# Edge rows of a graph network: gathered once per 128 sorted edges and loaded per tile by a table, instead of gathered per tile

## The reference

```
m   = relu(x3[src] @ We1[0:128] + x3[dst] @ We1[128:256] + be1)    # per edge
agg = segment_sum(m @ We2 + be2, dst)                              # per node
out = layernorm(x3 + relu([x3, agg] @ Wn1 + bn1) @ Wn2 + bn2)      # shortened
```

## Time and profile before

| | us |
|---|---|
| time, median of 3 runs | 4746.93 (4742.55 to 4747.23) |
| span of the profiled execution (no other time of it is given) | 7303.0 |
| POOL busy, 2706 instructions | 2658.9 |
| PE busy | 4076.2 |
| DVE busy | 3381.7 |
| ACT busy | 2340.3 |

### The profile page before, as it was taken

The page is one execution under the profiler, slowest core; times in us unless marked ns, Lnnn a source line. Parts: engine busy times, 40 slices in busy tenths (PEclk is TensorE's granted clock), DMA queues, the critical chain, the costliest instruction groups (busy, mean ns, idle before and its releaser), DMA issues. The chain is left out here.

```text
span 7303.0 us, 82736 instructions
## 1 busy us (share of the span) xinstructions
PE 4076.2 (56%) x24237; PEld 3354.5 (46%) x24238; DVE 3381.7 (46%) x7886; ACT 2340.3 (32%) x3120; POOL 2658.9 (36%) x2706
## 2 busy tenths in 40 slices
PE   4332641019981111117989798988672197666655
PEld 2111420007761101106778586858571197665644
DVE  4222540358970000106788776456451076555545
ACT  0000010005640000004555455557461075444433
POOL 4555157730017777770000000000427601444463
PEclk7665865559995555558999898989785598888777
DMA  9400000009970000116658287843444343444432
GB/s 376 155 0 0 0 2 0 0 23 334 368 250 0 0 0 0 28 25 222 232 189 293 96 293 214 296 162 95 132 125 124 97 139 98 132 132 130 130 95 67
DMA packets 364823, 923.20 MB, mean 126 GB/s; under 512 B 114026, under 2 KB 138716, under 8 KB 364531
## 3 DMA queue, kind: packets, MB, share of 16 engines
q1 hardware_dynamic: 214722, 650.09, 26.9%
q10 hardware_dynamic: 58609, 180.13, 6.4%
q0 software_dynamic: 91200, 89.42, 5.2%
HBM read 705.69 MB, written 213.71 MB: 126 GB/s over the span
## 5 line engine op out<-in xcount | busy, mean ns | idle before, releaser
L1741 POOL DMA_INDIRECT edges_halves<-local,gather_idx x832 | 854.9, 1027 | 791.7 <-SPq L372 505.4
L1680 POOL DMA_INDIRECT adj_t<-cell_val,cell_at x832 | 828.6, 996 | 465.2 <-issue 369.9
L862 PE MATMUL ps<-tiles_r,stage_r 128*128 128x512 f32 x2028 | 811.6, 400 | 158.2 <-issue 132.0
L1134 POOL DMA_INDIRECT big<-table,gather_idx x576 | 548.4, 952 | 832.3 <-DVE stage L1284 376.3
L869 PE MATMUL ps<-stage,big 128*128 128x130 f32 x4046 | 520.1, 284 | 370.3 <-issue 354.7
L1134 POOL DMA_INDIRECT x_fm<-table,gather_idx x384 | 370.2, 964 | 959.8 <-DMA table<-cell_at 689.7
L869 PEld LDWEIGHTS ps<-stage,big 128*128 128x128 f32 x4046 | 497.9, 199 | 388.5 <-issue 384.6
L2059 PE MATMUL ps<-big,ident_h 128*128 128x104 bf16 (+1 forms) x2880 | 359.7, 256 | 460.4 <-issue 459.7
L1253 PE MATMUL ps<-big,stage 128*128 x1920 | 356.2, 342 | 352.7 <-issue 189.3
L1319 PE MATMUL ps<-ident,big 128*128 128x128 f32 x260 | 73.3, 377 | 817.2 <-issue 768.2
L2442 DVE TENSOR_TENSOR big<-ps,stage 128x1248 bf16<-128x1248 f32 x192 | 270.7, 1451 | 519.5 <-remote 385.1
(11 more groups left out here) (482 smaller groups left out, 9007.8 us busy)
## 6 DMA issues: line engine op xcount, KB each, us to landing
onehot<-adj_t SPq DMA_DIRECT2D x332, 512.0 KB
big<-adj_t SPq DMA_DIRECT2D x332, 512.0 KB
onehot<-adj_s SPq DMA_DIRECT2D x170, 512.0 KB
adj_t<-rows ACTq DMA_DIRECT2D x13, 6656.0 KB
adj_s<-big ACTq DMA_DIRECT2D x157, 512.0 KB, 5.3
stage<-local_rows SPq DMA_DIRECT2D x120, 512.0 KB
big<-adj_s SPq DMA_DIRECT2D x84, 512.0 KB
x_fm<-adj_s SPq DMA_DIRECT2D x84, 512.0 KB
```

The lines of the kernel that those rows point to most:

```text
L862: nc.tensor.matmul(psum_fm(p, n)[:, 0:cut], upper_rows[:, k, :], tile[:, 0:cut], start=k == 0, stop=False, skip_group_check=True)
L1134: return nc.gpsimd.indirect_dma_start(out, None, table[0:N, :], bass.IndirectOffsetOnAxis(gather_idx[:, t:t + 1], 0))
L1680: nc.gpsimd.indirect_dma_start(out, bass.IndirectOffsetOnAxis(cells[:, c:c + 1], 0), cell_val[:, c:c + 1], None).then_inc(S(name), 16)
L1741: nc.gpsimd.indirect_dma_start(edges_halves, bass.IndirectOffsetOnAxis(slot_at[:, at:at + 1], 0), slot_val[:, at:at + 1], None).then_inc(h ...
```

## The change

All 960 gathers of tiles go. The rows of the table are gathered once for each of the 832 rows of sorted edges, in 52 sets of 16 (`GATHERS`, `GATHERED`), and each set is stored to HBM with one DMA of 1 MB. The first 19 sets (`EARLY`) are gathered beside the attention pass into SBUF of `x_fm`, the other 33 after its last weights are made, into SBUF of `big`, with no wait for the edge loop. In the edge stage SP loads each of the 8 tiles of a chunk with a DMA of its own, 128 x 512 bytes, two chunks ahead. Which set and which row of it a tile has, and how many stores must be done for a chunk, are int16 tables in partitions 1 to 3 of `block_of`; SP reads 1 + 8 + 8 of these values into registers per chunk. The tables are made beside the fifth pass and go through HBM (`tile_rows`) to their three partitions; SP waits for three DMAs at the end of that pass where it waited for one. SP also loads all 832 rows of sorted edges before that pass (`row_from`). All 120 chunks are alike, in order; the ring of rows keeps three slots, with a semaphore for each half.

```diff
-EARLY = 48
-EARLY_PAIRS = EARLY // 2
-DIRECT = CHUNKS - EARLY
-TURN = "DEDEDE"
+SLOTS = 3
+AHEAD = 2
+TURN = 2 * SLOTS
+GATHERED = 16
+GATHERS = EDGE_TILES // GATHERED
+EARLY = 19
...
+            eng.load(block_regs[eng, which], block_of[at:at + 1, bass.ds(CH * c, CH)])
+            return [eng.snap(r, min_val=0, max_val=most) for r in block_regs[eng, which]]
...
                 sp.dma_start(local_rows.rearrange("(g p) e -> p g e", p=P), pair_f).then_inc(S("local_stored"), 16)
-                sp.wait_ge(S("local_stored"), 16)
+                sp.dma_start(tile_rows.rearrange("(v g p) a -> p v (g a)", v=3, p=P), tile_row[:, :, :],
+                             allow_slow_non_contiguous=True).then_inc(S("local_stored"), 16)
+                sp.wait_ge(S("local_stored"), ROWS_IN + 32)
+                sp.dma_start(block_of[1:4, 0:T], tile_rows.rearrange("(v t) a -> v (t a)", v=3)[:, 0:T]
+                             ).then_inc(S("local_stored"), 16)
+                sp.wait_ge(S("local_stored"), ROWS_IN + 48)
...
-            for k in range(EARLY_PAIRS):
+            for k in range(GATHERS):
...
+                if k == EARLY:
+                    pool.wait_ge(S("weight_act"), KT * PASS_TURNS)
                 if k >= 2:
-                    wait(pool, early_stored, 16 * (k - 1))
-                for u in range(2 * CH):
-                    if u == CH // 2 and k > 0:
+                    pool.wait_ge(S("rows_stored"), 16 * (k - 1))
+                out = (early_sets if k < EARLY else late_sets)[k % 2]
+                for u in range(GATHERED):
+                    if u == GATHERED // 2 and k > 0:
                         store(k - 1)
...
-        def edge_pool(pool):
-            wait(pool, table_stored, 16 * GROUPS)
-            pool.wait_ge(S("weight_act"), KT * PASS_TURNS)
-            for k in range(DIRECT):
-                slot = k % HOT
-                if k >= HOT:
-                    pool.wait_ge(S("edge_pre"), 2 * direct_at(k - HOT) + 2)
                 for u in range(CH):
-                    gather(pool, row_ring[slot][:, u, :], (EARLY + k) * CH + u).then_inc(half_landed[2 * slot + u // 4], 16)
...
+            def rows_of(spot):
+                if not (spot.known and spot.i == 0 and spot.h < SLOTS):
+                    wait(sp, S("edge_pre"), 2 * (spot.u - SLOTS) + 2)
+                stored = sp.value_load(block_of[3:4, bass.ds(CH * spot.u + CH - 1, 1)], min_val=16, max_val=16 * GATHERS)
+                sets = tile_blocks(sp, spot.u, "set", 1, GATHERS - 1)
+                row = tile_blocks(sp, spot.u, "row", 2, GATHERED - 1)
+                sp.wait_ge(S("rows_stored"), stored)
                 for u in range(CH):
+                    sp.dma_start(spot.rows()[:, u, :], gathered_rows[bass.ds(sets[u], 1), :, bass.ds(row[u] * P, P)]
+                                 .rearrange("g p e -> p (g e)")).then_inc(landed_sem(2 * spot.slot + u // 4), 16)
+            for h in range(AHEAD):
+                rows_of(Spot(0, h))
             def body(spot):
                 wait(sp, S("hot_turned"), spot.u - 1)
-                sp.dma_start(targets[spot.par], local_rows[bass.ds(CH * spot.chunk, CH), :]...
+                sp.dma_start(targets[spot.par], local_rows[bass.ds(CH * spot.u, CH), :]...
-                if spot.h == 5 and not (spot.known and spot.i == LOOPS - 1):
-                    early(EARLY_SLOTS * (spot.i + 1), 0, spot.u - 4)
...
+                if not (spot.known and spot.i == LOOPS - 1 and spot.h + AHEAD >= TURN):
+                    rows_of(spot.after(AHEAD))
```

More of the change, by code:

```diff
@@ L387, in gnn @@
         targets_landed = [S(f"targets_landed{k}") for k in range(2)]
[L388 to L391, removed]
+        halves_written = [Count(S(f"at_written{k}"), 16 * sum(UNITS[k::2])) for k in range(2)]
+        gathered_in = [S(f"gathered_in{k}") for k in range(2)]
         turned_stored = [S(f"turned_stored{s}") for s in range(RING)]
@@ L445, in gnn @@
         targets = [stage[:, (4 + k) * CH * P:(5 + k) * CH * P] for k in range(2)]
[L446 to L450, removed]
+        assert 6 * CH * P <= NBP * W
+        late_sets = [big[:, NP + k * GATHERED * P:NP + (k + 1) * GATHERED * P] for k in range(2)]
+        slots_at = NP + 2 * GATHERED * P
+        row_ring = [out.rearrange("p (t f) -> p t f", f=P) for out in
+                    [rows_flat[:, CH * P:2 * CH * P]] + [big[:, slots_at + k * CH * P:slots_at + (k + 1) * CH * P] for k in range(2)]]
         HOTS = 3
@@ L974, in pair_locals, with row_sets @@
                 chain(dve)(last)
[L976 to L984, removed]
+            def row_sets():
+                for b, w in enumerate(ROW_SETS):
+                    if w != P:
+                        yield b, b + 1, w
+                yield 0, EDGE_TILES // P, P
@@ new lines, in row_sources @@
+            def row_sources():
+                one = chain(dve)
+                dve.wait_ge(S("local_stored"), ROWS_IN)
+                for lo, hi, w in row_sets():
+                    last = nc.vector.tensor_scalar(row_from[0:w, lo:hi, :], row_from[0:w, lo:hi, :], KEY_BITS, None,
+                                                   ALU.logical_shift_right)
+                one(last)
+                for lo, hi, w in row_sets():
+                    last = nc.vector.tensor_scalar(row_src[0:w, lo:hi, :], row_from[0:w, lo:hi, :], float(N - 1), None, ALU.min)
+                one(last)
@@ L1122, in edge_turns, with edge_pool @@
             turn(LOOPS - 1, True)
[L1123 to L1136 removed]
+        def edge_pool(pool):
             pool.wait_ge(S("pair_flipped"), 2)
@@ L1170, in edge_sp @@
[L1170 to L1180 removed]
+                    r = GATHERED * k + u
@@ L1244, in body @@
                 h = spot.par
-                blk = tile_blocks(pe, spot.chunk)
-                if not spot.x and spot.h == 0:
+                blk = tile_blocks(pe, spot.u)
+                if spot.h == 0:
                     wait(pe, node_kept, GROUPS if spot.nodes_done else spot.i)
@@ L1299, in body @@
                 if not spot.first:
-                    blk = tile_blocks(dve, spot.before().chunk)
+                    blk = tile_blocks(dve, spot.before().u)
                 gathered(spot)
@@ L1572, in _ @@
             end_stage(sp, nc.sync)
+            for k in range(2):
+                wait(sp, halves_written[k], 16 * SLW * SL // 2)
+            slots = edges_halves.rearrange("(r e) a -> r (e a)", e=P)
+            full = EDGE_TILES // P
+            sp.dma_start(row_from[:, 0:full, :], slots[0:full * P, :].rearrange("(g p) e -> p g e", p=P)).then_inc(S("local_stored"), 16)
+            if EDGE_TILES % P:
+                sp.dma_start(row_from[0:EDGE_TILES % P, full, :], slots[full * P:EDGE_TILES, :]).then_inc(S("local_stored"), 16)
             matrix_sp(4, sp)
@@ L1729, in _ @@
             pool.wait_ge(stage_end, ended["first"])
-            halves_written = [Count(S(f"at_written{k}"), 16 * sum(UNITS[k::2])) for k in range(2)]
             def sorted_there(n):
```

201 lines of the change are left out of this document (82 added, 119 removed).

## The result

The changed kernel takes 5097.65 us (median of 4 runs, 5095.81 to 5106.83), the kernel before 4747.08 beside it (4742.55 to 4754.35). The ratio is 1.0742, 95% interval 1.0727 to 1.0757: 350.6 us slower. The prediction was 5185 (4980 to 5420), slower at 0.90.

What follows compares the result with a forecast made beforehand. The prediction took DVE's chain of waits, not gathers, to bound the edge stage before, and SP's queue after. 4746.9 + 434 (edge stage) + 4 (tables and row load), early and late gathers 0, gave 5185 us, range 4980 to 5420.

Steps and rivals of the forecast that it cites:

- edge stage, after: Edge stage of the changed kernel: 120 SP turns of 10.1 us plus the last chunk's rest, 1234 us, +434.
- tables at the end of pass 5: End of the fifth pass: the tables' store and load end 3 to 4 us late; with the row load +4, bounds 0 and 15.
- SP becomes the engine that the stage waits for: Edge stage: SP's turn of 10.1 us (8.9 to 13.1) exceeds DVE's 6.53, so SP's queue holds up the stage.
- SP's turn, 10.1 us: Edge stage, per chunk: destinations load 0.53, single read 0.57, two reads of eight 4.28, eight issues 4.56, waits and loop 0.15.
- 120 turns of 6.53 before: Edge stage of the kernel before: 13 us, 120 turns of 6.53 us (784) and some 3 us, together 800 us.
- Gathers are not what bounds the stage: Edge stage of the kernel before: POOL waits for DVE, 376 us in all, so gathers are not the limit.
- Early gathers, 0: Attention pass: 384 gathers become 304; at 1.0 us each there was no stall before, so nothing to win.
- The bound of -47: Attention pass: at the traced pace the old early gathers end 47 us late, the new ones in time.
- Late gathers, 0 on the path: Edge stage: 576 gathers become 528, at most 696 us, under the 800 of before; POOL stays ahead, value 0.
- The first, SP keeps pace: Edge stage rival: register reads cost SP almost nothing, turn stays 6.53 us; 4704 us (chance 0.07) or 4751 (0.03).
- The second, the DMA engines: Edge stage rival: SP is cheap and the DMA engines bind at 7.3 us per turn, 4849 us; chance 0.08.
- The third, issue at 0.87: Edge stage rival: computed-address issues at 0.87 us, upper ends throughout, turn 13.1 us, time 5545 us; chance 0.12.

Runs made afterwards that it cites:

- experiment 2: Changed kernel with each chunk's rows loaded by one 512 KB DMA instead of eight of 64 KB, and one read of eight values gone: 4773.96 us, ratio 1.0071.
- experiment 3: Changed kernel without SP's 17 register reads per chunk; the eight 64 KB loads stay, at addresses from the loop index: 4780.8 us, ratio 1.0075.
- experiment 6: Changed kernel with rows asked for one chunk ahead instead of two, nothing else: 5049.74 us, ratio 1.0655.
- experiment 4: Changed kernel with gathered rows in one flat DRAM table, so one read of eight values per chunk instead of two: 4959.93 us, ratio 1.0453.
- experiment 5: Kernel of experiment 2 with rows asked for one chunk ahead instead of two: 4635.72 us, ratio 0.9764.
- experiment 8: Changed kernel without 512 of the 528 edge-stage gathers; those sets are stored stale, SP's work the same: 5088.62 us, ratio 1.0729.
- experiment 10: Kernel of experiment 4 with rows one chunk ahead, constant waits for stored sets, and ACT issuing local-destination loads three chunks ahead: 4643.51 us, ratio 0.9802.

## Why the prediction was right, and where it was not

From the two traces, in us, what the prediction gave and what was measured:

```
                                 forecast   measured
edge stage, before                  800        903   (4693.9 - 3791.0)
edge stage, after                  1234       1319   (5047.8 - 3729.1)
difference                         +434       +416
stall for the last early store        0        -76   (78.0 to 2.0)
tables at the end of pass 5          +4         +7   (ACT's wait there: 8.0 to 14.8)
not assigned, before that pass        0         +8
sum                                +438       +355   (spans 4739.2 and 5094.2)
```

*SP becomes the engine that the stage waits for.* Right. The waits run from DVE over PE and ACT to SP's load, and cheaper work on SP takes 320 us away (experiments 2 and 3).

*SP's turn, 10.1 us.* Right in sum, and in part by luck. The two reads of eight were given 2 x 1.92 and take 2 x 1.66; that is 0.21 us per value on SP where DVE has 0.23 and PE 0.24. A read does cost by the value, but not the same on every engine: 1.66 lies under the prediction's lower end of 1.83, and its value was 16% high. The Trainium skill's page Runtime: NRT & Kernel Launch, Instruction fetch mechanics, with about 200 ns per register, was nearer for the reads, but the turn of 9.4 that the prediction made with it was farther off. The eight issues were given 0.57 each and step by 0.58. The small terms (single read, arithmetic, waits, the load of destinations) were given 1.7 and take 2.0, which offsets part of the reads. The own sum is 9.96. What the prediction left out is what comes on top: 0.2 to 0.5 us for the ring of experiment 6, and beside POOL's traffic another 0.7 (10.82 against 10.08 in experiment 6), where single reads of eight take up to 4.2 us and single issues up to 1.46. So the mean is 10.69, and the stage after is 85 us longer than forecast. "A turn that is SP's instruction time" also hid the order in which SP works; it decided as soon as SP was cheaper (experiments 2 to 5).

*120 turns of 6.53 before.* A step that failed. The row was taken where early and gathered chunks alternate, and there the turn is 6.81 in the undisturbed trace, 27 us over 96 turns. The last 24 chunks have no early rows, the gathers bind them, and they take 248 us where the prediction had 173: the other 75. "Gathers are not what bounds the stage" holds for the first 96 turns only. The earlier trace rows show POOL waiting for DVE, but as one sum over the stage, and a sum doesn't show a part of another kind: the code has it, in the 24 spare chunks behind the loops.

*Early gathers, 0.* Failed. The prediction took 1.0 us per indirect DMA outside a trace, from a balance in which 512 us lay between the first two sets of scatters. In the undisturbed trace these are 1224.9 - 1166.5 = 58 us, and the scatters' own pace is (1166.5 - 85.8) / 831 = 1.30. The bound of -47 from the traced pace was on the right side and too small, since a set of before takes 22.4 us and not 21.1. (The end of the new sets "at about 620" doesn't follow from its figures either: 182 + 19 x 21.1 is 583.) The stall of before was 78, and 76 of it went. *The total.* The difference of the two stages, +434 and +416, agrees only because two errors cancel: the stage before was 103 us too short and the stage after 85, from causes that have nothing to do with each other. That is luck, though neither error alone would have carried the forecast out of its range. What is left, 87 us under the forecast, is mostly the stall. *Tables:* +7 in place of +4, inside 0 to 15.

*Late gathers, 0 on the path.* Right: POOL ends at 4390, and experiment 8 moves the time by 9.

*Rivals.* The first, SP keeps pace, needed under 0.02 us per value and found 0.21. The second, the DMA engines: experiment 10 moves the same bytes in 7.1 us per turn, 6.9 without the gathers, with the eight transfers of 64 KB and DVE as the bound. The page that it was weighed with (the Trainium skill, DMA: Bandwidth & Descriptors, Measured (HBM to SBUF), 0.95 us per such transfer, a row for DMAs issued from GpSimd) gave a turn of 12.6; these runs, with loads issued by SP, don't show it. The third, issue at 0.87, is refuted by the step of 0.58. That after's trace would show 7640 us was wrong: the crawl came with the one recording, and what made it is not known. (PE's crawl stands in slices 13 to 18 of the earlier trace rows, not 12 to 17; nothing hangs on it.)

## What to carry to other kernels

Before moving a choice of addresses from a gather into an issuing queue, sum that queue's turn, register reads by the value and issues by the piece (here 16 x 0.21 + 8 x 0.58 = 8 of 10 us), and set it against the stage's present turn. Then look at what stands behind each wait in that queue's order: in this kernel one chunk less of lead gave 138 us where the queue was otherwise cheap, and 48 where it was not. Measure a stage from its first to its last instruction in an undisturbed trace, and look for parts with another pattern before multiplying one turn by all.

## What the runs showed of the hardware

- In the changed kernel reads of eight registers take 1.66 us on SP (median of 240), 1.83 on DVE and 1.92 on PE, and single ones 0.26 on SP; beside POOL's gathers some on SP stretch, to 4.2 and 1.2 us, behind them none is over 1.68 and 0.43.
- A computed address costs SP's queue little: a step of 0.51 us with one register in it (experiment 4), 0.58 with two (the changed kernel).
- In the changed kernel's edge stage the granted clock of PE is 0.72 and 0.74, where the kernel before has 0.89 in its first 96 turns and 0.79 in the last 24; each is a mean over times at 1.2 and at 2.4 GHz. PE idles between its chunks there, and where the turn is near 7 again it is 0.89 and 0.90 (experiments 5 and 10, beside the gathers). Its products with Q take 408 ns on the mean, not 334. PE waits 530 us for ACT meanwhile; what the clock adds to the ring through PE, in experiments 2 to 4 above all, no run separates.
- A recording can be disturbed as a whole: the same kernel gave spans of 7303.0 and 4739.2 us, where its timed executions took 4735 to 4754.
